# Local attention: tiled products side by side on TensorE, Q scaled by GpSimd before its turn, exponentials without a scale

## The reference, cut to what matters

```python
h = shift_token(x)                       # the upper half of the channels moved by one token
q, k, v = split(h @ wqkv)                # 8 heads of 64
q = l2norm(q) * qs;  k = l2norm(k) * ksc
q, k = rotary_xpos(q, k)                 # q*cos*scale + rotate_half(q)*sin*scale, k likewise with 1/scale
sim = (8 * q) @ k.T                      # windows of 64 queries, keys of this and the last window
sim = where(mask, -inf, sim)             # causal, at most 64 back
attn = softmax(sim)
x = x + (attn @ v) @ wo
```

## Time and profile before

| what | us |
|---|---|
| median of 3 runs | 1315.5 |
| lowest and highest of the runs | 1315.08, 1316.87 |
| span of the profiled execution | 1360.5 |
| TensorE busy in it | 1171.3 (86%) |
| VectorE busy in it | 925.5 (68%) |
| ScalarE busy in it | 845.7 (62%) |
| GpSimd busy in it | 786.0 (58%) |

### The profile page before, as it was taken

The page is one execution under the profiler, slowest core; times in us unless marked ns, Lnnn a source line. Parts: engine busy times, 40 slices in busy tenths (PEclk is TensorE's granted clock), DMA queues, the critical chain, the costliest instruction groups (busy, mean ns, idle before and its releaser), DMA issues.

```text
span 1360.5 us, 36415 instructions
## 1 busy us (share of the span) xinstructions
PE 1171.3 (86%) x12703; PEld 877.6 (65%) x12704; DVE 925.5 (68%) x2483; ACT 845.7 (62%) x2476; POOL 786.0 (58%) x704
## 2 busy tenths in 40 slices
PE   5899898998979999789989899989688857768886
PEld 2676675776745555457668566676587845548775
DVE  7898669986856777588876888777533366663234
ACT  3899858998435555479985799954234425233344
POOL 6788348884663452288853778633666533265652
PEclk8999999999989999989999999998799989779998
DMA  7011100011000000000110001131355630135555
GB/s 222 18 24 26 28 16 9 22 34 27 17 3 3 4 3 3 2 9 21 25 30 16 19 20 26 26 90 32 109 171 161 182 108 0 32 94 155 173 172 167
DMA packets 69808, 78.21 MB, mean 57 GB/s; under 512 B 25094, under 2 KB 50501, under 8 KB 69509
## 3 DMA queue, kind: packets, MB, share of 16 engines
q1 hardware_dynamic: 64133, 64.70, 17.1%
q0 software_dynamic: 5504, 11.28, 2.9%
HBM read 54.60 MB, written 8.78 MB: 47 GB/s over the span
## 4 chain that ended last, share of the span: by engine, by line
PE 61%; DVE 11%; ACT 10%; DMA 6%; issue 5%; POOL 2%; SPq 1%; POOLq 1%; another core or an unknown queue 1%; ACTq 0%; DVEq 0%
PE bank L1849 10%; ACT pB L795 5%; PE bank L916 5%; DMA arena<-arena 4%; PE bank L1863 4%; PE bank L637 3%; PE bank L600 3%; PE bank L559 3%; PE bank L928 3%; PE bank L1515 3%; PE bank L1536 3%; PE bank L545 3%; PE bank L551 2%; PE bank L612 2%; PE bank L1547 2%
## 5 line engine op out<-in xcount | busy, mean ns | idle before, releaser
L2107 DVE SCALAR_TENSOR_TENSOR act_b<-bank,vec,gl 128x128 f32<-128x128 f32 x258 | 75.0, 345 | 178.4 <-PE bank L1849 72.3
L864 POOL TENSOR_TENSOR rn<-ss,mhalf 128x16 f32<-128x16 f32 x64 | 187.2, 2925 | 6.9
L1930 ACT ACTIVATE gl<-bank,vec 128x128 f32<-128x128 f32 x258 | 76.0, 365 | 120.2 <-PE bank L1849 96.9
L1849 PE MATMUL bank<-arena 128*128 128x128 f32 x1032 | 140.0, 288 | 3.4 <-DVE act_b L2107 1.9
L1849 PEld LDWEIGHTS bank<-arena 128*128 128x128 f32 x1032 | 130.6, 202 | 10.6 <-issue 7.2
L2179 POOL DMA_INDIRECT arena<-u_rows,inv_u x86 | 84.3, 981 | 71.4 <-remote 33.0
L795 ACT ACTIVATE pA<-bank,nb,rn 128x128 f32<-128x128 f32 x256 | 113.5, 484 | 3.4 <-DVE nb L726 3.4
L795 ACT ACTIVATE pB<-bank,nb,rn 128x128 f32<-128x128 f32 x256 | 113.3, 478 | 1.7 <-DVE nb L726 1.7
L850 POOL TENSOR_TENSOR arena<-arena 128x512 f32<-128x512 f32 x64 | 81.6, 1275 | 48.9 <-DVE nb L726 38.2
L2185 POOL DMA_INDIRECT y_rows<-stg,inv_u x86 | 84.5, 983 | 41.2 <-ACT stg L1937 20.8
L857 POOL TENSOR_TENSOR arena<-arena 128x512 f32<-128x512 f32 x64 | 81.3, 1270 | 43.0 <-DVE arena L689 16.3
(11 more groups left out here) (334 smaller groups left out, 3132.5 us busy)
## 6 DMA issues: line engine op xcount, KB each, us to landing
arena<-in_L_ffn_We SPq DMA_DIRECT2D x86, 384.0 KB
arena<-arena SPq DMA_DIRECT2D x64, 128.0 KB, 2.3
...
```

The lines of the kernel that those rows point to most:

```text
L864: pool.tensor_tensor(rn[:, q % 4, :, :], ss[:, 1, :].rearrange("p (a h) -> p a h", a=2), mhalf[:, :].rearrange("p (a h) -> p a h", a=2), A ...
L1849: m = pe.matmul(bank[q % 2][:, j * P:(j + 1) * P], we1[q][:, half * HR + j * P:half * HR + (j + 1) * P], xT[:, q, :], start=True, stop=True)
```

## The change

The steps get new orders:

- TensorE: k_proj(q+2), q_proj(q+2), turn(q-1, 0), out_proj(q-2), q_turn(q+1), turn(q-1, 1), sims(q), pv(q-1), v_proj(q), k_turn(q+1). So `sims` and `pv` stand side by side.
- VectorE: rope(q+2, K), norm(q-1, 1), rope(q+2, Q), result(q-2), squares(q+2), maxima(q), q_sum(q+2), norm(q, 0). `rope` no longer waits for the square. `squares` is two reductions of 128x512, each behind its own square. The product of the maxima with the norm is gone. `q_sum` is new here.
- ScalarE: exps(q-1, 1), qk_out(q, K), pt_out(q-1, 0), square(q+2, K), qk_out(q+1, Q), square(q+2, Q), pt_out(q-1, 1), exps(q, 0), o_out(q-1), v_out(q). `square` waits for rope of the same bank. The exponentials take the bare maxima as bias and have no scale.
- GpSimd: q_scaled(q), k_scaled(q), k_sum(q+1), power(q+1). `q_scaled` multiplies Q by its norm; the wait for the maxima is gone.

The projections now wait for the squares of the tile before and no longer for its rope. At the start of a block rope, squares and sum of Q of tile 1 come before step 0, and at its end the step NT+2 of VectorE falls away. `rn` has two buffers, no longer four, `nb8` is gone. Left out of the diff below: these declarations, the same shifts of the first pieces in `site_pe`, `site_act`, `site_pool` and for the first layer of each place in `site_dve`.

```diff
@@ -522,9 +521,9 @@
             return wqkv[:, l, k * INNER:(k + 1) * INNER]
 
         LoPe = namedtuple("LoPe", "step k_proj q_proj q_turn k_turn")
-        LoDve = namedtuple("LoDve", "step rope squares")
+        LoDve = namedtuple("LoDve", "step rope squares q_sum")
         LoAct = namedtuple("LoAct", "step square qk_out")
-        LoPool = namedtuple("LoPool", "step k_sum q_sum power")
+        LoPool = namedtuple("LoPool", "step k_sum power")
         X_AT = {1: 0, 3: 2 * NBATCH}
         RS_AT = {1: NCH, 3: NCH + 2 * NBATCH}
         LN_AT = {1: NCH, 3: NCH + 2 * NBATCH}
@@ -541,13 +540,13 @@
                 if l:
                     pe.wait_ge(s.xT_done, hb - NBATCH + q // 2 + 1)
                 if n:
-                    pe.wait_ge(s.rk_ab, n)
+                    pe.wait_ge(s.sqk_done, 2 * n - 1)
                 pe.matmul(BK[:, :], hT_of(q), wqkv_l(l, 1), start=True, stop=True).then_inc(s.k_ps, 1)
 
             def q_proj(q):
                 n = tb + q
                 if n:
-                    pe.wait_ge(s.rq_ab, n)
+                    pe.wait_ge(s.sqk_done, 2 * n)
                 pe.matmul(BQ[:, :], hT_of(q), wqkv_l(l, 0), start=True, stop=True).then_inc(s.q_ps, 1)
 
             def v_proj(q):
@@ -658,14 +657,14 @@
                     q_proj(q + 2)
                 if has(-1):
                     turn(q - 1, 0)
+                if has(-2):
+                    out_proj(q - 2)
+                if has(1):
+                    q_turn(q + 1)
+                if has(-1):
+                    turn(q - 1, 1)
                 if has(0):
                     sims(q)
-                if has(-1):
-                    turn(q - 1, 1)
-                if has(1):
-                    q_turn(q + 1)
-                if has(-2):
-                    out_proj(q - 2)
                 if has(-1):
                     pv(q - 1)
                 if has(0):
@@ -681,7 +680,7 @@
             def rope(q, k):
                 n = tb + q
                 bank = (BQ, BK)[k]
-                dve.wait_ge(s.sqk_done, 2 * n + 2 - k)
+                dve.wait_ge((s.q_ps, s.k_ps)[k], n + 1)
                 if n:
                     dve.wait_ge((s.qr_ready, s.kadd_ready)[k], n)
                 dve.tensor_tensor(heads(rab[:, 2 * k, :]), heads(bank[:, :]),
@@ -703,12 +702,13 @@
 
             def squares(q):
                 n = tb + q
-                dve.wait_ge(s.sqk_done, 2 * n + 2)
                 if n:
                     dve.wait_ge(s.ss_ready, n)
-                dve.tensor_reduce(ss[:, 0, :], sq[:, :, :].rearrange("p a (h d) -> p (a h) d", d=LD), AX_X, ALU.add)\
-                    .then_inc(s.ssk_raw, 1)
-                dve.wait_ge(s.ssk_raw, n + 1)
+                for k in (1, 0):
+                    dve.wait_ge(s.sqk_done, 2 * n + 2 - k)
+                    dve.tensor_reduce(ss[:, 0, k * LH:(k + 1) * LH], heads(sq[:, k, :]), AX_X, ALU.add)\
+                        .then_inc(s.ssk_raw, 1)
+                dve.wait_ge(s.ssk_raw, 2 * n + 2)
                 if n:
                     dve.wait_ge(s.rn_ready, n)
                 dve.tensor_scalar(ss[:, 1, :], ss[:, 0, :], 1e-24, None, ALU.max).then_inc(s.ss_ready, 1)
@@ -721,11 +721,11 @@
                     dve.tensor_reduce(mx8[:, par, x, :], BS[x][:, :].rearrange("p (u k) -> p u k", u=4), AX_X, ALU.max,
                                       negate=True)\
                         .then_inc(s.mx_ready, 1)
-                for x in range(2):
-                    dve.wait_ge(s.mx_ready, 2 * n + x + 1)
-                    dve.tensor_tensor(nb8[:, par, x, :], mx8[:, par, x, :],
-                                      rn[:, q % 4, 0, :].rearrange("p (u x) -> p x u", x=2)[:, x, :], ALU.mult)\
-                        .then_inc(s.smax_ready, 1)
+
+            def q_sum(q):
+                n = tb + q
+                dve.wait_ge(s.rq_ab, n + 1)
+                dve.tensor_tensor(rab[:, 0, :], rab[:, 0, :], rab[:, 1, :], ALU.add).then_inc(s.qadd_ready, 1)
 
             def result(q):
                 n = tb + q
@@ -736,29 +736,33 @@
                 def has(d):
                     return 0 <= q + d < NT
 
-                if has(-3):
-                    result(q - 3)
-                if has(1):
-                    rope(q + 1, 0)
-                    squares(q + 1)
+                if has(2):
+                    rope(q + 2, 1)
                 if has(-1):
-                    norm(q - 1, 0)
                     norm(q - 1, 1)
                 if has(2):
-                    rope(q + 2, 1)
+                    rope(q + 2, 0)
+                if has(-2):
+                    result(q - 2)
+                if has(2):
+                    squares(q + 2)
                 if has(0):
                     maxima(q)
-
-            return LoDve(step, rope, squares)
+                if has(2):
+                    q_sum(q + 2)
+                if has(0):
+                    norm(q, 0)
+
+            return LoDve(step, rope, squares, q_sum)
 
         def lo_act(act, l, pb):
             tb = pb * NT
 
             def square(q, k):
                 n = tb + q
-                if k == 1 and n:
-                    act.wait_ge(s.ssk_raw, n)
-                act.wait_ge((s.q_ps, s.k_ps)[k], n + 1)
+                if n:
+                    act.wait_ge(s.ssk_raw, 2 * n - k)
+                act.wait_ge((s.rq_ab, s.rk_ab)[k], n + 1)
                 act.activation(sq[:, k, :], (BQ, BK)[k][:, :], ACT.Square).then_inc(s.sqk_done, 1)
 
             def o_out(q):
@@ -787,14 +791,13 @@
             def exps(q, x):
                 n = tb + q
                 par = q % 2
-                act.wait_ge(s.smax_ready, 2 * n + x + 1)
+                act.wait_ge(s.mx_ready, 2 * n + x + 1)
                 if q > 1:
                     act.wait_ge(s.pT_ps, 2 * n + x - 3)
                 pr = probs(q, x)
                 for u in range(4):
                     m = act.activation(pr[:, u * P:(u + 1) * P], BS[x][:, u * P:(u + 1) * P], ACT.Exp,
-                                       bias=nb8[:, par, x, u:u + 1], scale=rn[:, q % 4, 0, 2 * u + x:2 * u + x + 1],
-                                       accum_out=den8[:, par, x, u:u + 1])
+                                       bias=mx8[:, par, x, u:u + 1], accum_out=den8[:, par, x, u:u + 1])
                 m.then_inc(s.exp_done, 1)
 
             def v_out(q):
@@ -809,24 +812,28 @@
                 def has(d):
                     return 0 <= q + d < NT
 
+                if has(-1):
+                    exps(q - 1, 1)
+                if has(0):
+                    qk_out(q, 1)
+                if has(-1):
+                    pt_out(q - 1, 0)
+                if has(2):
+                    square(q + 2, 1)
+                if has(1):
+                    qk_out(q + 1, 0)
                 if has(2):
                     square(q + 2, 0)
-                if has(-2):
-                    o_out(q - 2)
                 if has(-1):
                     pt_out(q - 1, 1)
-                if has(1):
-                    qk_out(q + 1, 0)
                 if has(0):
                     exps(q, 0)
-                    exps(q, 1)
-                if has(1):
-                    qk_out(q + 1, 1)
-                if has(3):
-                    square(q + 3, 1)
+                if has(-1) and has(0):
+                    o_out(q - 1)
                 if has(0):
                     v_out(q)
-                    pt_out(q, 0)
+                if q == NT + 1:
+                    o_out(NT - 1)
 
             return LoAct(step, square, qk_out)
 
@@ -849,19 +856,19 @@
                     pool.wait_ge(s.kr_ready, n)
                 pool.tensor_tensor(kadd[:, :], rab[:, 2, :], rab[:, 3, :], ALU.add).then_inc(s.kadd_ready, 1)
 
-            def q_sum(q):
+            def q_scaled(q):
                 n = tb + q
-                pool.wait_ge(s.rq_ab, n + 1)
+                pool.wait_ge(s.qadd_ready, n + 1)
+                pool.wait_ge(s.rn_ready, n + 1)
                 if n:
                     pool.wait_ge(s.qT_ps, n)
-                pool.tensor_tensor(qr[:, :], rab[:, 0, :], rab[:, 1, :], ALU.add).then_inc(s.qr_ready, 1)
+                pool.tensor_tensor(heads(qr[:, :]), heads(rab[:, 0, :]),
+                                   bc(rn[:, q % 2, 0, :].unsqueeze(2), [P, LH, LD]), ALU.mult).then_inc(s.qr_ready, 1)
 
             def power(q):
                 n = tb + q
                 pool.wait_ge(s.ss_ready, n + 1)
-                if q > 3:
-                    pool.wait_ge(s.exp_done, 2 * n - 6)
-                pool.tensor_tensor(rn[:, q % 4, :, :], ss[:, 1, :].rearrange("p (a h) -> p a h", a=2),
+                pool.tensor_tensor(rn[:, q % 2, :, :], ss[:, 1, :].rearrange("p (a h) -> p a h", a=2),
                                    mhalf[:, :].rearrange("p (a h) -> p a h", a=2), ALU.pow).then_inc(s.rn_ready, 1)
 
             def step(q):
@@ -869,15 +876,13 @@
                     return 0 <= q + d < NT
 
                 if has(0):
```

(13 more changed lines are left out.)

50 lines of the change are left out of this document (24 added, 26 removed).

## The result

The changed kernel takes **1367.74 us** (median of 4 runs, 1365.61 to 1370.32), against 1315.88 for the kernel before on the same chip: ratio **1.0398** [1.0374, 1.0421], 52 us slower. (A ratio is always to the kernel before on the same chip, and the brackets behind it hold its 95% interval.) The direction was forecast, the size was not: 1331 was predicted, and the range ended at 1352. The profiled execution of after lies among its runs (1365.61, span 1363.7). That of before lies 45 us above its own, and this lies behind the attention blocks: from the last exponentials of block 4 to the end it takes 475.6 us where after takes 428.0 (the indirect loads of line 2179 have 33.0 us of idle time with a releaser that the trace calls remote, those of after none).

A forecast was written before the change was run, and what follows sets the result against it. All four engines were taken as nearly full, with a new loop of waits between VectorE and ScalarE setting the tile. Loop +10.4, starts +8, ends -3.6 gave +15 us on 1315.5: 1331 us, range 1312 to 1352.

The forecast's parts named there:

- The loop: VectorE and ScalarE waiting on each other in each tile: 4.41 + 3.88 = 8.29 us against 8.09, +10.4 us.
- division 0.61: In VectorE's part of the loop, the division of half 1 of the probabilities takes 0.61 us.
- Starts: At block starts, first exponentials behind the second power: 0 to +3.6 us a block, taken as +2, +8 in all.
- Ends: At block ends, the last PV's 0.92 us wait for V's transfer goes: -0.9 us a block, -3.6 in all.
- Tiles 14 and 15 I leave as they are: The last tiles of a block, without a product of Q and K: no change in time counted.
- The exponentials: On ScalarE, each of eight exponentials loses its scale pointer: 0.09 us each, 0.72 us less a tile.
- Rival 2: On ScalarE, the accumulator read sets the exponentials' pitch and hides the pointer's price: loop 9.01 us, 1368 us; chance 0.10.
- Rivals 3 and 4: 3: pointer saving 0.12 us, 1318 or 1310 us, chance 0.16; 4: loop overlaps, TensorE's list sets pace, 1295 us, 0.09.
- The signs: Mid-block: tile 8.2 to 8.4 us, ScalarE idle 0.9 to 1.3, exponentials near 0.39, TensorE idle 0.6, transfer wait gone.

The follow-up runs named there:

- run 2: The changed kernel with GpSimd's scaling of K held back until VectorE's division of half 1 has ended: 1348.0 us, ratio 1.0251.
- Runs 10 and 11: The changed kernel, Q's sum in its own buffer, block's first scores, maxima and exponentials early: 1363.85 us; with GpSimd's scaling held back for VectorE's division too: 1349.38 us.
- runs 3 and 6: 3: the changed kernel with a scale pointer to ones in the exponentials, 1403.5 us; 6: the kernel before without its scale pointer, Q's norm left out, 1306.45 us.
- Run 4: The kernel before with TensorE's new order alone, everything else as before: 1567.35 us, ratio 1.1914.
- run 12: The kernel before with VectorE summing Q and GpSimd scaling it, no scale in the exponentials, orders of before: 1418.18 us, ratio 1.0402.
- Run 13: The kernel before with the new dependency alone, Q's turn moved behind the output projection and Q's copy between the exponentials' halves: 1374.58 us, ratio 1.0083.

## Why the prediction was right in its direction and wrong in its size

The sum had +14.8 us, the traces have +50.65. The 35.9 us between them are: loop 12.5, first intervals 7.3, starts 10.2, tiles 13 to 15 2.8, start to first power 1.75, ends 1.25.

- **The loop: right in its mechanism, one term mis-sized.** Its ScalarE side was right to 0.01. On the VectorE side "division 0.61" failed: it was taken from a place where GpSimd did not touch it, and measured 0.89. I had laid GpSimd's work out in time ("GpSimd's power starts at 3.8 and its scaling of Q ends at 7.8") and did not go on to the scaling of K, which runs from 7.8 on, that is into the next tile's division. A row of the kernel before could have warned me: VectorE's timeline at the start of block 2, where a division starts while GpSimd's sum of Q runs (212.64 to 213.90):

```profile
212.83 1.62 DVE L701 TENSOR_TENSOR pA<-pA,rden 128x512 f32<-128x512 f32 x1
```

  52 x (8.53 - 8.29) = 12.5 us of the miss; run 2 takes 20 us out and lands at 8.25.
- **Starts: wrong.** "I take +2" was near the middle between 0 and 3.6 a block; first power to first exponential costs +5.8, +3.5, +5.5 and +3.4, in all 18.2 for 8. Both terms failed. The way from the second power to the first exponential was taken at +3.6 a block, 14.3 in all, and is +19.0: 9.24, 8.25, 8.61 and 8.09 us for the forecast 6.5 (and 2.93 was read in block 2; blocks 1 and 3 have 4.66 in before). Missing were the longer power and the maxima of tile 0 behind the squares of tile 2, whose rotary products wait for scaled Q. The clock of 0.58 behind the idle 2.54 us is a small part: block 2 takes 0.2 us more than block 4, and block 1, at 0.58 too, 0.6 more than block 3, which has 1.00 there. That the second power would come 1 to 3 us earlier, 6.3 us in all, was true in blocks 2 and 4 alone (7.55 us behind the first in block 2, 9.35 before). In blocks 1 and 3 it comes 1.2 and 1.6 us later (12.41 and 10.51 for 11.19 and 8.92), behind normalization products that take longer (line 479: 3.52 us for 2.59, 2.06 for 1.32) and, in block 1, a wait of 1.44 us for the square of Q, which the change puts behind Q's rotary products. In all it is 0.8 us earlier. Runs 10 and 11 show that moving tile 0 alone does not help: the chain of powers goes on to tile 1.
- **Start to first power: left out.** +1.75 us, once. In block 1 the first squares now stand behind Q's two rotary products (1.20 us) and are two reductions (1.43 us for 1.21); the other 0.38 is there before these instructions.
- **First intervals: left out.** The 7.3 us of blocks 1 and 3 have no term in the sum. In block 1 the tables of the second layer's rotary embedding stand on VectorE between the two halves of tile 0's division, on which the turn, and in the new order the scores of tile 1 behind it, now wait (VectorE's and TensorE's timelines of after):

```profile
43.43 0.77 DVE L439 TENSOR_TENSOR arena<-rot_sb,qs_row 128x128 f32<-128x128 f32 x1
...
46.97 1.77 DVE L700 TENSOR_TENSOR pA<-pA,rden 128x512 f32<-128x512 f32 x1
...
48.80 1.12 PE L611 MATMUL bank<-ident_sb,pA 128*128 128x128 f32 x4 [3.44 <-DVE pA L700]
```

In run 2 what the two intervals have over two tiles falls from 5.1 to 2.1 us in block 1 and from 2.1 to 0.3 in block 3. So much of it, too, goes with GpSimd's instructions: divisions take 1.77 here, and 1.38 and 1.78 in block 3's second interval. In block 3's first interval the maxima wait 0.86 us for the scores, at a granted clock of 0.57 (627 to 631 us) where run 2 has 1.00; no run took the clock's part by itself.
- **Ends: right in sign.** Between the last exponentials and the next block's power 0.7 to 0.8 us went, 2.35 for 3.6 (the sum had four ends, the traces can be compared in three). The last PV's wait of 0.92 us for the transfer is gone, as forecast, but the same PV now waits 0.69 us for the copy of the probabilities. "Tiles 14 and 15 I leave as they are": they cost 0.3 to 0.9 a block, 2.8 in all.
- **The exponentials: right.** 484 ns became 386, pitch 0.434 became 0.344; the pointer is worth 0.09 in runs 3 and 6 too. The Trainium skill ("ScalarE: Activation LUTs", What ACT_TABLE_LOAD costs) has about 93 ns for a pointer, and the trace agrees.
- **Rival 2 gave 1368 and is false.** It came out at the measured time by chance: the accumulator read does not set the pitch, 0.34 with the read inside.
- **Rivals 3 and 4 are false.** The saving was 0.09, not 0.12. TensorE's list never set the pace of after: in a stretch of 110.7 us it is busy 103.1, and in the steady tiles PV waits 0.50 us for the copy of the probabilities. By the Trainium skill's rule that a change of tiling drains TensorE ("TensorEngine Tiling (Array Packing)", Key Properties), at the 0.19 us of the earlier trace rows, the kernel would have been 10 us faster by an estimate. It is 52 us slower, and no run shows what the saved change is worth. Run 4, which was to price it, ran into another wait.
- **Which half costs.** The dependency alone, in the orders of before, costs as much (1.0402) as the whole change (1.0398): the power and the scaling stand ahead of Q's turn. The change's new orders have a loop of 8.53 us in place of that one of 9.00, 21 us less over the 44 later intervals, and give most of it back: the first two intervals of the blocks take 9.5 us more than in run 12, the starts 3.6, the first power comes 1.9 later. Run 13 cut the loop more cheaply, so the dependency does not cost 4% by itself; it costs what the orders around it make of it.
- **The signs.** ScalarE's wait of 1.06 us, records of 0.386 us, TensorE's idle time of 0.6 us a tile and the transfer's wait gone were all as forecast; the tile of 8.53 lies above the 8.2 to 8.4.
